# GNN kernel: fewer sorted tiles, their leftovers packed into gathered steps (100 sorted and 320 gathered steps a pass)

## The chip, the cores and the metric

The kernel runs on one core of one Trainium2 chip. The metric is the device time of one execution in microseconds (us). The kernel before took 2686.7 us (median of 3 runs, 2684.65 to 2692.53).

## The reference, cut to what matters

There are 3125 nodes with 128 features and 50000 directed edges, sorted by destination. Sources are uniform; destinations are `3125 * u**2`, so low nodes get many edges. First a gated network runs five steps over the graph, then a layer norm. Then three edge layers run, and it is these that the change touches:

```python
def _gnn_layer(edge_index, x, edge_attr, norm, We, be, Wn, bn):
    src, dst = (edge_index[0], edge_index[1])
    parts = [x[src], x[dst]]
    if edge_attr is not None:
        parts.append(edge_attr)
    e = relu(concatenate(parts, axis=-1) @ We + be)
    msg = e * norm[:, None]
    agg = segment_sum(msg, dst, num_segments=x.shape[0])
    x_new = relu(concatenate([x, agg], axis=-1) @ Wn + bn)
    return (x_new, e)
x, e = _gnn_layer(edge_index, z, None, norm, We0, be0, Wn0, bn0)
x, e = _gnn_layer(edge_index, x, e, norm, We1, be1, Wn1, bn1)
x, e = _gnn_layer(edge_index, x, e, norm, We2, be2, Wn2, bn2)
```

A second layer norm of the result plus its input is the output.

## The kernel before, in words

Nodes are cut into 25 windows of 128. Edges are cut into tiles of 128 and, since they are sorted by destination, each piece of a tile that falls into one destination window is a **step**; there is room for 416 steps. `x[src] @ We_a` and `x[dst] @ We_b` are made once per node in a node stage (P and Q); P goes to memory as `p_dram`, and both stay on the chip as three bfloat16 parts (`p_parts`, `q_parts`).

An **edge pass** (`edge_pass`, one per layer, called pass 0, 1 and 2 here) works in slots of four steps (`QUAD`). There are two kinds of slot.

- A **gathered** slot, here R, covers the later steps. GpSimd fetches P's row of every edge by an indirect DMA, one per step (L1496), into one of 7 row buffers. TensorE adds Q by a one-hot matrix, 3 matmuls a step (L1585), VectorE adds the gathered rows (`add`, L1714), ScalarE applies relu (L1657).
- A **sorted** slot, here S, covers tiles whose edges share both the source window and the destination window. Their P comes from the chip too: 3 matmuls a step with the source's one-hot matrix (L1578) and 3 with the destination's (L1585), so nothing is gathered. VectorE makes both one-hot matrices of the four tiles in one operation (`paired_hot`, L1695), and relu reads the PSUM bank.

Passes 1 and 2 also add the previous layer's e times a weight (L1589, 2 matmul records a step); passes 0 and 1 turn e and store it (L1600). Every slot ends with a weighted one-hot product per step (`turn_and_sum`, L1607), which VectorE adds to the destination window's sums (`gather_up`, L1721). TensorE's order is written out: the products of slot q, then the turning and summing of slot q-1. VectorE's is: `add` of slot q (or the pair of one-hots of the next sorted slot), then `gather_up` of slot q-1 with the weighted one-hots of slot q+1 between. A row buffer is given back when the slot that used it is summed, and only then does GpSimd gather into it.

The kernel before has 38 sorted slots and 76 gathered ones in the fixed order S R R, so 114 slots a pass. The windows' numbers that the matmuls need are read into registers once in three slots (`lists`, L1469).

Which edge goes to which sorted tile is worked out at the start (`sort_on_dve` and its matmuls in `step_tables`): the first 112 steps are counted by source window and destination window (a block), every block gets as many tiles as it needs, rounded up, and each edge's place is the first place of its block plus its rank (`block_rank`, summed by L340). The places are used by an indirect scatter in the next stage (L625). The register loads, the table loads and the one-hot rows of the first steps follow in `node_stage`. If the sorted tiles did not suffice, a loop at the end of each pass (`overflow`, L1503 and on) would treat further tiles one by one.

## Time and profile before

| | |
|---|---|
| median of 3 runs | 2686.7 us |
| the profiled execution, its own time | 2711.26 us |
| its span, first to last instruction | 2709.1 us |
| TensorE matmul busy | 2123.5 us (78%) |
| VectorE busy | 1447.8 us (53%) |
| GpSimd busy | 1068.0 us (39%) |
| ScalarE busy | 675.5 us (25%) |
| mean granted TensorE clock | 0.880 |

The stages by the profile: tables and sorting 0 to 70 us, the adjacency matrix 70 to 400, the gated steps to 938, a layer norm and the first node stage to some 1022, then pass 0 to 1513, pass 1 to some 2115, pass 2 to 2670, each followed by a node stage. Busy shares are averages over these stages. Matmul records are modelled at their end, so a busy TensorE is not one at its peak, and an idle engine costs nothing unless another waits for it.

### The profile page before, as it was taken

How to read it: one execution, taken by the hardware profiler on the slowest of the kernel's cores; microseconds unless marked ns; L12 is line 12 of the kernel's file. 1: busy time of each engine (PE TensorE's matmuls, PEld its weight loads, DVE VectorE, ACT ScalarE, POOL GpSimd, SP SyncE). 2: the span in 40 equal slices, each digit the busy share in tenths (PEclk: the TensorE clock that was granted, in tenths of full speed). 3: DMA queues.
4: the chain of work that ended last, by engine and by line, in shares of the span. 5: the costliest groups of instructions: out<-in, count | busy, mean ns of one | idle time of the engine just before them, and what ended most of it. 6: DMA issues, size and time to landing. Idle time of an engine off the chain costs nothing. (4 is left out here: it accounts for less than half of the span.)

```text
span 2709.1 us, 50361 instructions
## 1 busy us (share of the span) xinstructions
PE 2123.5 (78%) x14516; PEld 1514.4 (56%) x14516; DVE 1447.8 (53%) x4548; ACT 675.5 (25%) x1344; POOL 1068.0 (39%) x1086
## 2 busy tenths in 40 slices
PE   7777769999999726777777558888889458888885
PEld 5112124444444425666776348877878357777773
DVE  6888751322323255666666425555556336566565
ACT  0245751221212131222222312222222301111111
POOL 0544410000000035666664165555553266666650
PEclk7667779999999867889788769999999679999997
DMA  2023560000000043434443135555554134444431
GB/s 80 21 59 72 88 64 1 0 0 0 0 0 0 24 175 116 119 115 118 116 117 110 46 107 166 167 166 166 170 168 159 53 88 115 117 118 117 120 110 38
DMA packets 188937, 242.82 MB, mean 90 GB/s; under 512 B 53218, under 2 KB 115069, under 8 KB 188077
## 3 DMA queue, kind: packets, MB, share of 16 engines
q1 hardware_dynamic: 155852, 179.60, 22.9%
q0 software_dynamic: 32864, 60.32, 9.3%
q8 instruction: 135, 2.21, 0.3%
q14 instruction: 86, 0.70, 0.1%
HBM read 150.92 MB, written 69.26 MB: 81 GB/s over the span
## 5 line engine op out<-in xcount | busy, mean ns | idle before, releaser
L1496 POOL DMA_INDIRECT rows<-p_dram,src_i x912 | 899.4, 986 | 561.1 <-PE psum L1607 230.5
L1721 DVE TENSOR_TENSOR agg_t<-psum,agg_t 128x128 f32 x1368 | 390.8, 286 | 493.9 <-PE psum L1607 208.2
L1589 PE MATMUL psum<-w_c,before 128*128 128x128 f32 x1824 | 419.3, 310 | 18.9 <-issue 18.6
L882 PE MATMUL psum<-adj,parts 128*128 (+2 forms) x1750 | 340.0, 352 | 5.3 <-ACT agg L961 4.4
L1705 DVE TENSOR_SCALAR hot_w<-col_f,dst_loc,weight 128x128 f32<-128x128 f32 x912 | 323.9, 357 | 0.3
L1657 ACT ACTIVATE rows<-rows 128x512 f32<-128x512 f32 x228 | 143.6, 630 | 720.1 <-DVE rows L1714 459.7
L1585 PE MATMUL psum<-q_parts,hot_all 128*128 x2736 | 283.4, 221 | 29.3 <-issue 28.4
L1589 PEld LDWEIGHTS psum<-w_c,before 128*128 128x128 f32 x1824 | 289.3, 199 | 22.2 <-issue 22.2
L662 PE MATMUL psum<-src_hot,dst_hot 128*128 128x391 f16 x586 | 230.7, 439 | 77.5 <-ACT psum L684 26.7
L1607 PE MATMUL psum<-hot_w,rows 128*128 128x128 f32 x1824 | 270.2, 292 | 26.5 <-issue 24.9
L1578 PE MATMUL psum<-p_parts,pair_hot 128*128 x1368 | 194.2, 245 | 105.5 <-DMA before<-e_dram 49.4
L1262 POOL MEMSET agg_t<- 128x3200 f32 x3 | 8.3, 2765 | 664.4 <-POOLq L1010 607.4
L1607 PEld LDWEIGHTS psum<-hot_w,rows 128*128 128x128 f32 x1824 | 243.4, 205 | 33.8 <-issue 30.3
L882 PEld LDWEIGHTS psum<-adj,parts 128*128 128x128 f16 x1750 | 153.2, 98 | 190.9 <-issue 23.7
L1585 PEld LDWEIGHTS psum<-q_parts,hot_all 128*128 128x128 bf16 x2736 | 219.6, 99 | 51.9 <-issue 39.4
L1585 PE MATMUL psum<-q_parts,pair_hot 128*128 x1368 | 225.5, 246 | 15.6 <-issue 14.9
L1714 DVE TENSOR_TENSOR rows<-psum,rows 128x512 f32<-128x512 f32 x228 | 156.6, 687 | 138.5 <-remote 119.9
L1578 PEld LDWEIGHTS psum<-p_parts,pair_hot 128*128 128x128 bf16 x1368 | 134.5, 109 | 140.3 <-issue 121.8
L830 DVE SCALAR_TENSOR_TENSOR gate_room<-psum,b_h,gate_room 128x512 f32<-128x512 f32 (+1 forms) x35 | 23.9, 683 | 348.9 <-ACT gate_room L968 348.9
L662 PEld LDWEIGHTS psum<-src_hot,dst_hot 128*128 128x128 f16 x586 | 59.2, 101 | 249.1 <-issue 249.1
L644 DVE TENSOR_SCALAR src_hot<-gate_room 128x391 f16<-128x391 f16 x586 | 167.7, 332 | 53.2 <-PE psum L662 39.9
L625 POOL DMA_INDIRECT records<-record_of,place_i x112 | 125.6, 1122 | 158.6 <-PE psum L662 158.1
(248 smaller groups left out, 2547.2 us busy)
## 6 DMA issues: line engine op xcount, KB each, us to landing
e_dram<-after SPq DMA_DIRECT2D x228, 256.0 KB
before<-e_dram SPq DMA_DIRECT2D x228, 256.0 KB
adj<-stage SPq DMA_DIRECT2D x196, 97.8 KB
pair_rows<-sorted_rows SPq DMA_DIRECT2D x114, 128.0 KB
rows<-p_dram,src_i POOLq DMA_INDIRECT x912
hot_all<-dst_rows SPq DMA_DIRECT2D x1, 3584.0 KB
hot_all<-dst_rows SPq DMA_DIRECT2D x1, 3072.0 KB
hot_all<-dst_rows SPq DMA_DIRECT2D x1, 2048.0 KB, 7.5
```

The lines of the kernel that those rows point to most:

```text
L644: nc.vector.tensor_scalar(src_hot[:, s % MOVES, :], span_h, place_f[:, s:s + 1], None, ALU.is_equal).then_inc(src_on, 1)
L662: nc.tensor.matmul(psum[:, bass.ds(bank, 1), 0:SPAN], dst_hot[:, s // HOT_BATCH % BATCHES, s % HOT_BATCH, :], src_hot[:, s % MOVES, :], st ...
L882: mm = nc.tensor.matmul(psum[:, AGG_BANK, 0:n_cols], parts[:, w, part, :], adj[:, w, cols], start=(w == 0 and part == 0), stop=(w == WINDO ...
L1496: nc.gpsimd.indirect_dma_start(out=rows[:, b % ROWS, m * D:(m + 1) * D], out_offset=None, in_=p_dram, in_offset=bass.IndirectOffsetOnAxis( ...
L1578: nc.tensor.matmul(o, hots[0], t["p_parts"][:, bass.ds(values[m], 1), part, :], start=(part == 0), stop=False)
L1585: mm = nc.tensor.matmul(o, hot, t["q_parts"][:, bass.ds(window, 1), part, :], start=(part == 0 and i is None), stop=(part == 2 and e_befor ...
L1589: mm = nc.tensor.matmul(o, before[:, q % BEFORE, m * P:(m + 1) * P], w_c[:], start=False, stop=True)
L1607: mm = nc.tensor.matmul(psum[:, A_BANKS[q % len(A_BANKS)], m * P:(m + 1) * P], e[:, m * D:(m + 1) * D], hot_w[:, q % 2, m, :], start=True, ...
L1657: nc.scalar.activation(e_of(q), source, ACT.Relu).then_inc(e_on, 1)
L1705: nc.vector.tensor_scalar(hot_w[:, q % 2, m, :], keep["col_f"][:], of, weight, ALU.is_equal, ALU.mult).then_inc(hot_on, 1)
L1714: nc.vector.tensor_tensor(row, psum[:, E_BANKS[q % len(E_BANKS)], 0:WIDE], row, ALU.add).then_inc(added, 1)
L1721: nc.vector.tensor_tensor(a, psum[:, A_BANKS[q % len(A_BANKS)], m * P:(m + 1) * P], a, ALU.add).then_inc(agg_on, 1)
```

## The change

Only the first 104 steps are sorted. A block now gets full tiles, and one more if 64 edges or more are left over; fewer than 64 are left out of the sorted tiles. What is left out of all blocks of one destination window is packed side by side into tiles of that window, 8 tiles in all (`LEFT_TILES`), which are treated as gathered steps. So a pass has 25 sorted slots and 80 gathered ones (312 of the steps as before, plus the 8 packed tiles), 105 in all. They are mixed evenly: of each 21 slots 5 are sorted, with 4, 3, 3, 3 and 3 gathered slots behind them.

For this the sorting gives every edge two keys instead of one (the first tile of its block with its rank, and where its leftovers start with how many tiles its block fills), takes them apart with shifts and masks, and chooses the place. The window numbers are in two tables now, read once in two sorted slots and once in four gathered ones.

```diff
-SORT_STEPS = 112
-SORT_QUADS = 38
+SORT_STEPS = 104
+SORT_QUADS = 25
 SORT_TILES = SORT_QUADS * QUAD
-REST_STEPS = STEPS - SORT_STEPS
+LEFT_TILES = 8
+HELD_TILES = LEFT_TILES + SORT_TILES
+FULL_FROM = 64
+REST_STEPS = STEPS - SORT_STEPS + LEFT_TILES
-ALL_TILES = 737
+ALL_TILES = 236
+RANKS, FILLS = 14, 9
...
     dve.wait_ge(block_sizes, 1)
-    after(nc.vector.tensor_scalar(tiles_i[0:W, :], psum[...], float(P - 1), None, ALU.add))
+    after(nc.vector.tensor_scalar(tiles_i[0:W, :], sizes, float(P - FULL_FROM), None, ALU.add))
     after(nc.vector.tensor_scalar(tiles_i[0:W, :], tiles_i[0:W, :], 7, None, ALU.logical_shift_right))
     after(nc.vector.tensor_copy(tiles_f[0:W, :], tiles_i[0:W, :]))
+    after(nc.vector.scalar_tensor_tensor(out=left[0:W, :], in0=tiles_f[0:W, :], scalar=-float(P), in1=sizes, ...))
+    after(nc.vector.tensor_scalar(left[0:W, :], left[0:W, :], 0.0, None, ALU.max))
+    v.on(nc.vector.tensor_reduce(row_sums[0:W, 0:1], tiles_f[0:W, 0:W], AXIS_X, ALU.add))
+    after(nc.vector.tensor_reduce(row_sums[0:W, 1:2], left[0:W, 0:W], AXIS_X, ALU.add))
+    after(nc.vector.tensor_scalar(left_i[0:W, :], row_sums[0:W, 1:2], float(P - 1), None, ALU.add))
+    after(nc.vector.tensor_scalar(left_i[0:W, :], left_i[0:W, :], 7, None, ALU.logical_shift_right))
+    v.on(nc.vector.tensor_copy(left_tiles[0:W, :], left_i[0:W, :]))
...
+    for key in range(2):
+        if key:
+            dve.wait_ge(vec, done["rank_key0"])
         for i, a in enumerate(range(0, W, CHAINED)):
             ...
+        done[f"rank_key{key}"] = v.on(nc.vector.tensor_reduce(
+            rank_key[:, key, :], block_rank[:].rearrange("p k s -> p s k"), AXIS_X, ALU.add))
+    after(nc.vector.tensor_copy(key_i[:], rank_key[:]))
+    ... (20 more operations of 128 x 104, most of which wait for the one before)
     v.on(nc.vector.tensor_tensor(keep["place_i"][:], place[:], spare[:], ALU.add))
...
     pe.wait_ge(vec, done["step_base"])
-    for i in range(chains):
-        a, n, _ = below(i)
-        for k in range(n):
-            mm = nc.tensor.matmul(psum[:, i, k * S:(k + 1) * S], row_of[:, a + k, :],
-                                  step_base[0:W, :], start=False, stop=(k == n - 1))
+    for key in range(2):
+        for i in range(chains):
+            a, n, _ = below(i)
+            ...
+            for k in range(n):
+                mm = nc.tensor.matmul(psum[:, j % CHAIN_BANKS, k * S:(k + 1) * S], row_of[:, a + k, :],
+                                      step_base[0:W, key, :], start=(key == 1), stop=(key == 1 or k == n - 1))
...
     # the first node stage
+    sp.wait_ge(tabs, 80)
     for i in range(1, len(HOT_CHUNKS) - 1):
         load_hot(sp, i)
...
+    dve.wait_ge(keep["sorted_got"], 16)
+    for to, f in ((t["src_i"], 3), (t["dst_loc"], 1), (t["weight"], 2)):
+        nc.vector.tensor_copy(to[:, STEPS - SORT_STEPS:REST_STEPS],
+                              keep["sorted_in"][:, 0:LEFT_TILES, f]).then_inc(turned_on, 1)
...
     # the edge pass
+    order, nth_of = [], []
+    for q in range(SLOTS):
+        kind = q * SORT_QUADS % SLOTS < SORT_QUADS
+        nth_of.append(order.count(kind))
+        order.append(kind)
+    slots = {kind: [q for q in range(SLOTS) if order[q] == kind] for kind in (True, False)}
+    AT_A_TIME = {True: 2, False: 4}
...
+    def lists(values, q, engine):
+        i, n = nth_of[q], AT_A_TIME[order[q]]
+        if i % n == 0:
+            ... (16 values from pair_i or rest_i)
...
-                if q >= len(E_BANKS) and i is not None:
+                if q >= len(E_BANKS) and order[q - len(E_BANKS)]:
                     pe.wait_ge(e_on, q - len(E_BANKS) + 1)
```

## Rows read from the trace of the kernel before

**Rows 1.** Windows: busy of PE, PEld, DVE, ACT, POOL, clock, DMA share, GB/s.

```profile
52.00:64.00 12.00, 11.65 (x57) 11.44 (x58) 9.31 (x34) 0.00 (x0) 0.00 (x0) 0.50 0.00 0
...
1037.00:1505.00 468.00, 357.34 (x3156) 322.39 (x3156) 304.60 (x1090) 129.32 (x227) 276.35 (x276) 0.86 0.39 114
...
1575.00:2104.00 529.00, 446.26 (x4053) 407.38 (x4053) 285.94 (x1020) 127.86 (x228) 285.35 (x293) 0.94 0.53 158
...
2190.00:2662.00 472.00, 386.04 (x3584) 344.61 (x3583) 284.71 (x1016) 69.96 (x113) 274.93 (x279) 0.98 0.39 111
```

**Rows 2.** Source line L1657, relus of gathered slots, passes 0, 1, 2: min/median/max ns.

```profile
L1657 ACT ACTIVATE rows<-rows x76: 629/629/631, 1037.1 to 1499.1; 128x512 f32<-128x512 f32 x76
...
L1657 ACT ACTIVATE rows<-rows x76: 629/630/632, 1601.0 to 2096.0; 128x512 f32<-128x512 f32 x76
...
L1657 ACT ACTIVATE rows<-rows x76: 629/630/633, 2198.2 to 2656.8; 128x512 f32<-128x512 f32 x76
```

**Rows 3.** Timeline of TensorE, slots in passes 0, 1, 2: start us, us, work.

```profile
1304.50 0.53 PE L1578 MATMUL psum<-p_parts,pair_hot 128*128 x3
...
1308.04 0.83 PE L1585 MATMUL psum<-q_parts,hot_all 128*128 x12
...
1316.02 0.53 PE L1578 MATMUL psum<-p_parts,pair_hot 128*128 x3
...
1320.64 0.83 PE L1585 MATMUL psum<-q_parts,hot_all 128*128 x12
...
1329.54 0.53 PE L1578 MATMUL psum<-p_parts,pair_hot 128*128 x3
...
1862.51 0.56 PE L1578 MATMUL psum<-p_parts,pair_hot 128*128 x3 [0.62 <-issue]
...
1867.20 0.33 PE L1585 MATMUL psum<-q_parts,hot_all 128*128 x3
...
1875.65 0.57 PE L1578 MATMUL psum<-p_parts,pair_hot 128*128 x3 [0.46 <-DMA before<-e_dram]
...
2412.39 0.48 PE L1578 MATMUL psum<-p_parts,pair_hot 128*128 x3 [0.26 <-issue]
...
2417.30 0.33 PE L1585 MATMUL psum<-q_parts,hot_all 128*128 x3
...
2424.85 0.35 PE L1578 MATMUL psum<-p_parts,pair_hot 128*128 x2 [0.23 <-issue]
```

**Rows 4.** Waits between 1050 and 1480 us: total us, times, longest us.

```profile
POOL rows L1496 <- PE psum L1607: 74.6, 54, 1.8
POOL rows L1496 <- issue: 62.5, 204, 0.4
```

**Rows 5.** Source line L1496, the gathers of pass 0.

```profile
L1496 POOL DMA_INDIRECT rows<-p_dram,src_i x303: 938/944/1402, 999.7 to 1472.1; - x152
```

**Rows 6.** Timeline in pass 0, a gather beside the pair of one-hots.

```profile
1307.56 0.74 DVE L1695 TENSOR_SCALAR pair_hot<-pair_rows,lane_f 128x1024 bf16<-128x1024 uint8 x1
1307.72 1.39 POOL L1496 DMA_INDIRECT rows<-p_dram,src_i  x1 [0.30 <-issue]
```

**Rows 7.** Source line L1469, the loads of window numbers into registers.

```profile
L1469 PEldq TENSOR_LOAD <-list_i x114: 1101/1106/1882, 997.8 to 2645.6; - x114
```

**Rows 8.** Timeline of the sorting, 39 to 68 us.

```profile
39.52 0.27 DVE L280 SCALAR_TENSOR_TENSOR valid<-dst_e,inside 128x112 f32<-128x112 f32 x1
39.82 0.27 DVE L282 SCALAR_TENSOR_TENSOR src_key<-src_win,valid 128x112 f16<-128x112 int32 x1
...
52.35 11.00 PE L543 MATMUL psum<-step_base,row_of 25*128 25x112 f32 x50 [0.35 <-DVE step_base L327]
...
63.80 4.85 DVE L340 TENSOR_REDUCE place<-block_rank 128x112 f32<-128x2800 f32 x1
```

**Rows 9.** Timeline behind pass 0: the last sums, then the node stage.

```profile
1501.47 1.59 DVE L1721 TENSOR_TENSOR agg_t<-psum,agg_t 128x128 f32 x4 [0.91 <-PE psum L1607]
...
1513.02 0.29 DVE L1770 TENSOR_TENSOR agg_t<-psum,agg_t 128x128 f32 x1 [1.45 <-PE psum L1640]
```

More of the change, by code:

```diff
@@ new lines, in sort_on_dve @@
+            after(nc.vector.tensor_scalar(at_i[:, 2, :], at_i[:, 0, :], P - 1, None, ALU.bitwise_and))
+            after(nc.vector.tensor_tensor(tile_f[:], base[:], at_i[:, 1, :], ALU.add))
+            after(nc.vector.tensor_scalar(shift_f[:], tile_f[:], float(LEFT_TILES), past[:, 1:2], ALU.is_ge, ALU.mult))
+            after(nc.vector.scalar_tensor_tensor(out=shift_f[:], in0=shift_f[:], scalar=-float(LEFT_TILES),
+                                                 in1=is_left[:], op0=ALU.add, op1=ALU.mult))
@@ L1453, in edge_pass, with pair_slot @@
         E_BANKS, T_BANKS, A_BANKS = (0, 1, 2), (3, 4), (5, 6, 7)
+        order, nth_of = [], []
[5 more added lines that the diff above has]
+        AT_A_TIME = {True: 2, False: 4}
         def sorted_of(q):
-            return q // 3 if q % 3 == 0 else None
+            return nth_of[q] if order[q] else None
         def rest_of(q):
-            return q // 3 * 2 + q % 3 - 1
+            return nth_of[q]
         def slot_of(b):
-            return b // 2 * 3 + b % 2 + 1
-        def lists(i, first, engine):
-            _, values = nc.values_load_multi_w_load_instructions(
-                keep["list_i"][0:1, i, first:4 * QUAD], engines=(engine,), min_val=0, max_val=WINDOWS - 1,
-                skip_runtime_bounds_check_because="a window's number is a count of at most all the windows but one")
-            return values
+            return slots[False][b]
+        def pair_slot(i):
+            return slots[True][i]
+        def lists(values, q, engine):
+            i, n = nth_of[q], AT_A_TIME[order[q]]
+            if i % n == 0:
+                if order[q]:
+                    table = keep["pair_i"][0:1, i:min(i + n, SORT_QUADS), :, :].rearrange("p i f m -> p (i f m)")
+                else:
+                    table = keep["rest_i"][0:1, i * QUAD:min(i + n, REST_QUADS) * QUAD]
+                _, values[order[q]] = nc.values_load_multi_w_load_instructions(
+                    table, engines=(engine,), min_val=0, max_val=WINDOWS - 1,
+                    skip_runtime_bounds_check_because="a window's number is a count of at most all the windows but one")
+            per = 2 * QUAD if order[q] else QUAD
+            return values[order[q]][i % n * per:(i % n + 1) * per]
         def overflow(engine):
             return nc.values_load(keep["over_i"][0:1, 0:1], engines=(engine,), min_val=0,
-                                  max_val=ALL_TILES - SORT_TILES)
+                                  max_val=ALL_TILES - HELD_TILES)
         def over_window(engine):
@@ L1730, in _ @@
                     weighted_hot(q, m)
+            loaded = {}
             for q in range(SLOTS):
```

204 lines of the change are left out of this document (135 added, 69 removed).

## The prediction, made before the result was known

> **What bounds the kernel now.** I read the page first: its span by stages says that three edge passes take some 1470 us of 2709, and the change reaches little else. Then the windows of the passes [rows 1]: the busiest engine in each is TensorE (357 of 468 us, 446 of 529, 386 of 472), with GpSimd behind it. GpSimd's busy time leaves out the issue gap between gathers. One gather is 276.35/276 = 1.00 us in pass 0 and 0.97 to 0.99 in the others [rows 1], and 62.5/204 = 0.31 us passes before most [rows 4], so a gathered slot takes GpSimd 4 x 1.31 = 5.2 us in pass 0 and 4 x 1.29 = 5.15 in the others. In each triple S R R that is 10.4 us of about 12.4, and the rest it waits for a row buffer, that is for TensorE's sums (74.6 us in 430) [rows 4]. So the gathers follow the slots and don't set their pace. TensorE's in-order stream, with VectorE's adds and ScalarE's relus hung into it, does.
>
> The pace comes from the relus of the gathered slots [rows 2]. The first is slot 1 and the last slot 113, 112 slots apart: 462.0/112 = 4.13 us a slot in pass 0, 495.0/112 = 4.42 in pass 1, 458.6/112 = 4.09 in pass 2. The 15 to 40 us before the first of them (first rows and tables) don't depend on the slots' number.
>
> **What a slot of each kind costs** is to be read from where TensorE starts its products [rows 3]. From the start of S to that of the next R is S's share; from there to the next S are two R. Pass 0: S 3.54 and 4.62, mean 4.08; R (7.98 + 8.90)/4 = 4.22. Pass 1: S 4.69, R 8.45/2 = 4.23. Pass 2: S 4.91, R 7.55/2 = 3.78. The sums 12.5, 13.1 and 12.5 agree with three times the pace. A sorted slot has 12 more matmuls than a gathered one, so it is a little dearer where TensorE is fullest.
>
> **The passes.** Each loses 13 S and gains 4 R.
> - Pass 0: -13 x 4.08 + 4 x 4.22 = -36.2 us.
> - Pass 1: -13 x 4.69 + 4 x 4.23 = -44.1.
> - Pass 2: -13 x 4.91 + 4 x 3.78 = -48.7.
>
> Together -129.0. With the mean slot instead (9 fewer at 4.13, 4.42, 4.09) it would be -113.8; I take the split, because TensorE's products are what differs.
>
> Does GpSimd keep up? In 21 slots there will be 16 gathered ones: 16 x 5.2 = 83 us of gathers against 5 x 4.08 + 16 x 4.22 = 88 us of slots in pass 0, 82 against 91 in pass 1, 82 against 85 in pass 2. It does, with 3 to 10% left. The longest run is 4 gathered slots and there are 7 buffers, so a run is served out of what was fetched during the sorted slot before it. The whole of pass 0's 320 gathers takes 320 x 1.31 = 419 us from its first issue at 999.7 [rows 5], so to 1419; the forecast end of the pass is about 1465. That lead of GpSimd is the cover; the rivals say what it costs if it is gone.
>
> VectorE: 304.6 us busy in 468 [rows 1]; a gathered slot gives it an add instead of a pair of one-hots, about the same, and 9 slots fewer a pass. ScalarE is at 28%. The SP queue issues 9 fewer stores and loads of e a pass and 13 fewer pair loads. Loads of window numbers [rows 7], 1.10 us each on TensorE's queue: 13 + 20 = 33 a pass instead of 38, beside the sums already issued; I count nothing (a bound: 15 fewer x 1.1 = 16 us gained if none is hidden). VectorE reads 16 numbers now instead of 12, in time when it waits for sums. TensorE's wait for the slot three before now asks for relu only where the bank held a sorted slot; it never waits longer than before.
>
> **The sorting** is on the path: the next stage begins only when it has ended. The 50 matmul records of L543 took 11.0 us [rows 8] at a granted clock of 0.50 [rows 1], 1.2 GHz, though TensorE was busy 11.65 of 12 us. There will be 100 of 104 columns, about 20.5: +9.5 to 11, I take 10.2. A second reduction (4.85 us) [rows 8] runs after them, the first is hidden beneath them: -0.35 for the smaller size. Behind it 22 more VectorE operations. Two dependent ones start 0.30 apart [rows 8]; some 15 wait so, the rest at about half: 5.1. Ahead of the matmuls seven more small operations on the block sizes, three small products and two more base products, each at 0.1 to 0.3: 2.9. In sum +17.9, I say +17.5; from 12 (if the clock rises in the longer run) to 23.
>
> **The rest** costs nothing by its cover: the scatter has 104 steps instead of 112 inside a stage that TensorE and VectorE fill; zeroing the records falls from 737 tiles to 236, beside the sorting; three small copies in the first node stage fall into VectorE's wait for the first products; SP's new wait for five small tables stands behind four stores of P issued much later; the last chunk of one-hot rows is 0.5 MB longer and needed half a pass later. If the covers failed, I put 5 us on them together.
>
> **The overflow loop** ran one turn behind each pass: the profile has its last sum after pass 0 [rows 9]. A count over the reference's edges (seed 0) gives 146 sorted tiles of 152 now, so its body runs once even with nothing left over. For the change the same count gives 99 full tiles of 100 and 880 edges left, which pack into 8 tiles of 8. So one turn again, no difference.
>
> **Sum**, against the profiled execution: 2711.3 - 129.0 + 17.5 = 2599.8 us. The median of the runs is 0.9909 of that execution; the same share gives 2576.
>
> **Rivals.**
> - *A sorted slot costs others more than its own time.* Its 24 products stand in TensorE's order before the sum that frees a row buffer and that VectorE waits for. If this delay is what makes the R behind it dear, R falls too. The floor is GpSimd: 16 x 5.15 us in 21 slots, 3.92 a slot, 404 us for 103 slots, against 462, 495 and 459 today: -204. Half way between forecast and floor is -166, so 2711 - 166 + 17 = 2562, 2539 as a median. For it: pass 0 had R's between 3.6 and 6.9 apart in two neighbouring triples. Against: with this many R's GpSimd's waits would have to vanish altogether.
> - *The sorted slot was GpSimd's breathing space.* 5 to 10% is little left; if buffers come late in each run and half the gain is lost in waits for rows, the passes give -65: 2711 - 65 + 17 = 2663, 2639.
> - *The gathers become the bound: slower.* Place: GpSimd, beside VectorE's one-hots. A gather that ran beside the pair of one-hots took 1.39 us instead of 0.94 [rows 5, 6]. If all did, one would be 1.39 + 0.31 = 1.70 and a pass 544 us, against 1472.1 - 999.7 = 472 now: +72 a pass, +216 + 17, about 2917. It decides from 472/320 = 1.48 us a gather on; 1.31 is measured. The pairs become fewer by a third, the weighted one-hots stay at four a slot. Against it: the median gather is 944 ns with VectorE 65% busy [rows 1, 5].
> - *The clock.* It is 0.86 granted in pass 0 and 0.94 and 0.98 in the others [rows 1]. Fewer products a slot leave TensorE emptier. If passes 1 and 2 fell to 0.86, their TensorE time, 446 and 386 us before, would be longer by 9% and 14%: after the cut about +37 and +47, half of it on the path, +42: 2642, 2618 as a median.
> - *More overflow* (the count wrong): each tile over costs one more turn, 1513.31 - 1503.06 = 10.3 us [rows 9], three times a run, +31; four such tiles would eat the gain.
>
> Two rules of the Trainium skill speak against the change. "SBUF — State Buffer", section "SBUF: two separate sides", says that GpSimd can't write the descriptors of a DMA while VectorE runs an operation that takes the port pair they share. By that rule each of the weighted one-hots would hold the gathers up, which is the third rival at its full price; the one long gather beside the pair agrees, the median doesn't. "TensorE: Matmul & The Clock Gate", Part 1, says that an idle TensorE falls to half its clock; by it the fourth rival is the case to fear, and pass 0, the emptiest pass, has the lowest clock. By the same rule the sorting's matmuls would have run at full clock once busy; the row at 0.50 shows that they didn't.
>
> **How the numbers follow.** The forecast, 2545 to 2610, has 0.55. The dearer sorted slot has 0.20, the lost breathing space 0.10, the clock 0.08, gathers as the bound 0.05, more overflow 0.02 (half of it still faster). Predicted: 2576. The range is to hold 8 in 10: its low end, 2525, takes in three quarters of the first rival; its high end, 2635, takes in the clock and half of the breathing space. A measurement of this kernel can tell about 0.3% (8 us) from no change. Slower are gathers as the bound 0.05 and half of more overflow 0.01, so 0.06; 0.02 of the breathing space and the clock I give to no measurable change, and the rest, 0.92, is faster.
>
> **What would show it.** Relus of gathered slots: 80 a pass, from the first to the last about 426, 451 and 410 us, a slot at 4.0 to 4.4. GpSimd's waits for L1607 down to a fifth; gathers at 0.94 to 1.0 us, 960 of them. The scatter's first piece at 91 us instead of 73.5, since the stage begins so much later. One turn of the overflow loop a pass. Wrong would be: VectorE's add waiting for rows most of the time, a clock under 0.9 in pass 2, or gathers at a median above 1.2 us.

## The result, and the profile after

The kernel after takes 2755.9 us (median of 4 runs, 2752.33 to 2758.83), beside 2685.8 (2684.65 to 2692.53) for the kernel before: the ratio is 1.0249 [1.0235, 1.0263], slower. The forecast was 2576, range 2525 to 2635. The profiled executions are 2711.26 and 2752.33 us, so the trace explains 41 us of the 70; the rest is that the profiled execution of before was 1% above its median and that of after 0.1% below.

One thing has to be known first. The 18 experiments ran in five groups, each on a chip of its own beside the kernel before. In three groups (e, f, h) that kernel took 2383 to 2385 us, in two (g, k) 2713 to 2714, and in the result 2686. All executions of it in one group agree. So there are two conditions of the machine, called **prompt** (2384) and **late** (2686 to 2714) here. Whether they belong to the chip or to the hour isn't known, since no chip was used twice. The result is of the late one, and so is the profile that the prediction rests on. The change is slower in both.

Windows of the kernel after, with the columns of [rows 1]: the sorting, then passes 0, 1 and 2.

```profile
52.00:68.00 16.00, 15.54 (x72) 14.64 (x72) 10.94 (x38) 0.00 (x0) 0.00 (x0) 0.50 0.00 1
1054.00:1531.00 477.00, 345.09 (x2774) 298.43 (x2774) 281.21 (x1006) 115.44 (x208) 283.25 (x292) 0.82 0.35 104
1609.00:2111.00 502.00, 410.06 (x3596) 367.16 (x3596) 259.85 (x927) 117.37 (x208) 296.24 (x307) 0.94 0.52 154
2200.00:2699.00 499.00, 394.19 (x3180) 349.99 (x3180) 261.18 (x928) 64.87 (x105) 286.52 (x298) 0.85 0.36 100
```

TensorE has 9 slots fewer than in [rows 1] and is busy for 345, 410 and 394 us instead of 357, 446 and 386; in pass 2 it is busy longer with less to do, at a granted clock of 0.85 instead of 0.98. The relus of gathered slots, as in [rows 2], show what that means for the passes.

```profile
L1772 ACT ACTIVATE rows<-rows x80: 629/629/631, 1055.1 to 1530.6; 128x512 f32<-128x512 f32 x80
L1772 ACT ACTIVATE rows<-rows x80: 629/630/632, 1631.9 to 2110.8; 128x512 f32<-128x512 f32 x80
L1772 ACT ACTIVATE rows<-rows x80: 629/630/632, 2211.8 to 2698.8; 128x512 f32<-128x512 f32 x80
```

| first to last such relu, us | pass 0 | pass 1 | pass 2 | sum |
|---|---|---|---|---|
| before [rows 2] | 462.0 | 495.0 | 458.6 | 1415.6 |
| after, forecast | 426 | 451 | 410 | 1287 |
| after | 475.5 | 478.9 | 487.0 | 1441.4 |
| us a slot (before 112, after 103 intervals) | 4.13 to 4.62 | 4.42 to 4.65 | 4.09 to 4.73 | |

The rest is as forecast: the first of them begins 18.0 us later than before, and what lies between and behind the passes is 2.4 us shorter. So 18.0 + 25.8 - 2.4 = 41.4 us, the difference of the spans (2750.5 and 2709.1).

The gathers in the view of the line and in the waits between 1050 and 1480 us, the counterparts of [rows 4, 5]:

```profile
L1612 POOL DMA_INDIRECT rows<-p_dram,src_i x960: 938/944/1509, 1016.4 to 2673.4; - x192
...
POOL rows L1612 <- issue: 69.7, 228, 0.4
POOL rows L1612 <- PE psum L1723: 49.6, 21, 9.8
POOL rows L1612 <- remote: 45.0, 25, 2.3
DVE rows L1829 <- PE psum L1701: 16.2, 9, 10.2
```

A gather costs what it did, 944 ns at the median. GpSimd still waits for row buffers, 49.6 + 45.0 = 94.6 us in 46 pauses, though more rows are wanted. In before it was 74.6 us [rows 4] and one more line of that view, together 89.7 us in 68 pauses:

```profile
POOL rows L1496 <- remote: 15.1, 14, 1.4
```

The longest wait of an add for TensorE is 10.2 us, which is two slots.

**Where TensorE's results are.** One place of pass 0 in after, by engine. First TensorE:

```profile
1160.36 0.83 PE L1701 MATMUL psum<-q_parts,hot_all 128*128 x12
...
1164.80 0.47 PE L1701 MATMUL psum<-q_parts,pair_hot 128*128 x3
1166.47 0.22 PE L1694 MATMUL psum<-p_parts,pair_hot 128*128 x1 [1.20 <-issue]
1167.19 0.22 PE L1694 MATMUL psum<-p_parts,pair_hot 128*128 x1 [0.50 <-issue]
1167.91 0.22 PE L1694 MATMUL psum<-p_parts,pair_hot 128*128 x1 [0.50 <-issue]
1169.29 0.46 PE L1701 MATMUL psum<-q_parts,pair_hot 128*128 x3 [1.16 <-issue]
```

The timeline of VectorE, the adds, and then of GpSimd:

```profile
1160.74 0.68 DVE L1829 TENSOR_TENSOR rows<-psum,rows 128x512 f32<-128x512 f32 x1
1169.36 0.69 DVE L1829 TENSOR_TENSOR rows<-psum,rows 128x512 f32<-128x512 f32 x1 [5.87 <-remote]
```

```profile
1157.96 0.94 POOL L1612 DMA_INDIRECT rows<-p_dram,src_i  x1 [1.54 <-PE psum L1723]
1159.20 0.94 POOL L1612 DMA_INDIRECT rows<-p_dram,src_i  x1 [0.30 <-issue]
...
1165.44 0.94 POOL L1612 DMA_INDIRECT rows<-p_dram,src_i  x1 [0.30 <-issue]
1166.69 0.95 POOL L1612 DMA_INDIRECT rows<-p_dram,src_i  x1 [0.30 <-issue]
1169.76 0.94 POOL L1612 DMA_INDIRECT rows<-p_dram,src_i  x1 [2.12 <-remote]
```

The twelve products of a gathered slot are recorded as done at 1161.19. The add that reads them begins at 1169.36, 8.2 us later, with VectorE idle for 5.87 us before it. In that time GpSimd issues eight gathers without a pause, 1157.96 to 1167.64, and TensorE's next matmuls start only every 0.72 us, though nothing that the profile shows holds them. When the eight are issued, all moves again. I call it a slow stretch when three or more times in a row the next matmul starts at least 0.55 us after the last, with no wait for another engine. After has 20, 3 and 13 of them in passes 0, 1 and 2; before has 2, 1 and 1, at the passes' starts. The matmuls' record and their reader's start lie up to 9.0 us apart in after and up to 5.5 in before; in the mean, without the first seven gathered slots of a pass, it is 2.3 us in after and 3.0 in before. So results are late in before too, and more evenly.

In before GpSimd pauses after each four. Its timeline:

```profile
1149.31 0.94 POOL L1496 DMA_INDIRECT rows<-p_dram,src_i  x1 [1.03 <-PE psum L1607]
1150.55 0.94 POOL L1496 DMA_INDIRECT rows<-p_dram,src_i  x1 [0.31 <-issue]
1151.80 0.96 POOL L1496 DMA_INDIRECT rows<-p_dram,src_i  x1 [0.30 <-issue]
1153.06 0.94 POOL L1496 DMA_INDIRECT rows<-p_dram,src_i  x1 [0.30 <-issue]
1155.62 0.94 POOL L1496 DMA_INDIRECT rows<-p_dram,src_i  x1 [1.61 <-PE psum L1607]
```

In after, behind the 28 gathers that need not wait for a buffer, 24 series of pass 0, none of pass 1 and 13 of pass 2 have eight. How this is tied to the slots' time is what the experiments ask.

### The profile page after: what moved, and what is told of

Read it like the earlier page. It is cut to its first block and busy times, and to the rows that moved or that the text cites. A ratio compares the mean times of both kernels' runs of the same rounds, so it can differ in the third digit from the quotient of the medians.

```text
span 2750.5 us, 46647 instructions
## 1 busy us (share of the span) xinstructions
PE 2092.9 (76%) x13351; PEld 1467.4 (53%) x13351; DVE 1396.1 (51%) x4356; ACT 648.6 (24%) x1299; POOL 1087.8 (40%) x1126
## 5 line engine op out<-in xcount | busy, mean ns | idle before, releaser
L1612 POOL DMA_INDIRECT rows<-p_dram,src_i x960 | 927.9, 967 | 568.9 <-issue 238.3
L1836 DVE TENSOR_TENSOR agg_t<-psum,agg_t 128x128 f32 x1260 | 357.1, 283 | 519.0 <-DMA records<-pad 180.9
L1701 PE MATMUL psum<-q_parts,hot_all 128*128 x2880 | 346.8, 240 | 105.7 <-issue 94.6
L1723 PE MATMUL psum<-hot_w,rows 128*128 128x128 f32 x1920 | 304.5, 295 | 76.3 <-issue 65.9
L1701 PEld LDWEIGHTS psum<-q_parts,hot_all 128*128 128x128 bf16 x2880 | 260.5, 109 | 158.0 <-issue 138.4
L1820 DVE TENSOR_SCALAR hot_w<-col_f,dst_loc,weight 128x128 f32<-128x128 f32 x960 | 336.6, 353 | 0.8
L1723 PEld LDWEIGHTS psum<-hot_w,rows 128*128 128x128 f32 x1920 | 264.4, 207 | 94.6 <-issue 83.7
L1694 PE MATMUL psum<-p_parts,pair_hot 128*128 x900 | 120.5, 231 | 98.1 <-issue 63.4
L1772 ACT ACTIVATE own<-psum 128x512 f32<-128x512 f32 x75 | 44.8, 597 | 480.6 <-remote 419.0
L1716 PE MATMUL psum<-ident,rows 128*128 128x128 f32 x640 | 110.6, 299 | 58.9 <-ACT rows L1772 40.2
(300 smaller groups left out, 2423.0 us busy)
```

Source lines behind the costliest of these rows:

```text
L1612: nc.gpsimd.indirect_dma_start(out=rows[:, b % ROWS, m * D:(m + 1) * D], out_offset=None, in_=p_dram, in_offset=bass.IndirectOffsetOnAxis( ...
L1694: nc.tensor.matmul(o, hots[0], t["p_parts"][:, bass.ds(values[m], 1), part, :], start=(part == 0), stop=False)
L1701: mm = nc.tensor.matmul(o, hot, t["q_parts"][:, bass.ds(window, 1), part, :], start=(part == 0 and i is None), stop=(part == 2 and e_befor ...
L1723: mm = nc.tensor.matmul(psum[:, A_BANKS[q % len(A_BANKS)], m * P:(m + 1) * P], e[:, m * D:(m + 1) * D], hot_w[:, q % 2, m, :], start=True, ...
L1772: nc.scalar.activation(e_of(q), source, ACT.Relu).then_inc(e_on, 1)
L1820: nc.vector.tensor_scalar(hot_w[:, q % 2, m, :], keep["col_f"][:], of, weight, ALU.is_equal, ALU.mult).then_inc(hot_on, 1)
```

## The experiments

Gathered relus, first to last in each pass, stand behind each time. Ratios are to before on the same chip. A time without a ratio is of one execution. "Old rows" means that the add takes what lies in the row buffer.

### Group e, prompt machine (before 2383.4)

**e1**: the kernel after in the order S R R as long as there are sorted slots, then 30 R.

```diff
-            kind = q * SORT_QUADS % SLOTS < SORT_QUADS
+            kind = q % 3 == 0 and q < 3 * SORT_QUADS
```

> What is tested: in the kernel after the change TensorE has stretches, about one to each sorted slot in passes 0 and 2, in which one matmul starts only every 0.70 to 0.72 us with no wait on anything the profile shows. Here only the order of the slots changes: S R R 25 times (75 slots, the order of the kernel before), then the other 30 gathered slots in one run. Theory order (a run of three or four gathered slots lets TensorE's stream fall into such a stretch at the next sorted slot): the first 75 slots of a pass go at 4.1 to 4.4 us each as before, and the passes lose about what I forecast, so 2590 to 2640 us. Theory loads (the window numbers are now read into registers at other places and times than once ahead of each triple): the order is not the cause, the stretches stay, 2730 to 2770 us. Theory gathers (more gathers a slot disturb TensorE): the stretches gather in the last 30 slots, which then take over 5 us each; in sum 2700 to 2770.

Measured: 2423.0, ratio 1.0171 [1.0154, 1.0188]; 379.5, 397.1, 394.6. That is the time of after itself on a prompt machine (f2 below, 2420.7), so the order is worth nothing here. All three ranges that were expected had a late machine in view.

**e2**: TensorE takes window numbers fixed in the program, so it loads no registers.

```diff
-                products(q, lists(loaded, q, mybir.EngineType.PE))
+                products(q, [4 * (q % 5) + m for m in range(2 * QUAD)])
```

> The kernel after, with TensorE's products reading a window of P and Q that is fixed in the program instead of one from a register, so that TensorE's queue has neither the register loads nor the register operations of the passes; the products have the same sizes, but are with the wrong windows. If the stretches hang on the registers (theory loads, or the sequencer's register work in general), they are gone and the passes take at most 3.9 us a slot: 2450 to 2600 us. If they come from the order or from the gathers, they stay: 2700 to 2760 us.

Measured: 2420.7; 381.8, 396.2, 395.4. Nothing again.

**e3**: only the first 7 gathered slots of a pass fetch rows (84 gathers in all, later slots add old rows).

```diff
-            for b in range(REST_QUADS):
-                if b >= ROWS:
-                    pool.wait_ge(summed, slot_of(b - ROWS) + 1)
+            for b in range(ROWS):
```

> The kernel after, in which GpSimd gathers only the first seven slots of each pass; the later gathered slots work on what lies in the row buffers. The 960 gathers become 84. Theory gathers: the stretches go, and a slot takes 4 us or less: 2550 to 2620 us. Theories order and loads: they stay, and since the rows landed some 30 us ahead anyway the time is within 1% of 2756 us.

Measured: 2217.2; 311.1, 350.4, 304.8. So 200 us lie with the gathers.

**e4**: the kernel before with its window numbers loaded by kind, as after does (two sorted or four gathered slots at once).

> The kernel before, with one part of the change alone: the window numbers are read into registers as the kernel after does it (8 for each of two sorted slots at once, 4 for each of four gathered slots at once, each time where the first of them is used) instead of 16 once ahead of each S R R. Nothing else is changed; 38 loads a pass become 38 (19 and 19). Theory loads: the stretches appear here too and the kernel gets slower by 50 us or more, 2730 to 2800 us. Theory order or gathers: within 0.5% of 2686 us.

Measured: 2377.6, 0.9974 [0.9964, 0.9985]; 364.3, 395.4, 378.3. The one part of the change that gains, 6 us by the medians. In the traces it is pass 1 that gets shorter (395.4 against 408.7 in f1). It was not run on a late machine.

### Group f, prompt machine (before 2385.1): the four corners

**f1** and **f2** are before and after unchanged; **f3** and **f4** are before and after with e3's edit.

> The kernel before, unchanged, for its trace beside the others of this group. In the first group it ran at 2383 us, 300 us faster than in the runs that the prediction rests on, and the traces there show GpSimd issuing one gather every 1.25 us without a break. Theory gathers (where TensorE's products end as soon as their records say, the gathers set the pace: 304 x 1.25 = 380 us a pass): the time is about 2383 us, passes of 368, 400 and 381 us from the first relu to the last, GpSimd waiting under 20 us for TensorE in all three. If it falls into the condition of the first runs instead: 2686 us, slots of 4.1 to 4.6 us, and matmuls whose results come up to 5 us after their records.

> The kernel after, unchanged. Theory gathers: 320 x 1.25 = 400 us a pass, 16 more gathers are +20 us a pass where they bound already (passes 0 and 2), in pass 1 less, and +18 us for the sorting: 2420 to 2435 us beside 2383, ratio 1.016 to 1.022. Theory stretches (slow stretches of TensorE at the sorted slots are what costs, wherever it runs): ratio 1.025 with such stretches in the trace. My forecast of 0.96 would need the passes to follow TensorE's slots.

> The kernel before, gathering only the first seven slots of each pass (84 gathers instead of 912). With the same edit of the kernel after (passes of 314.6, 353.2 and 307.8 us for 25 sorted and 80 gathered slots) it gives the price of a slot to TensorE and VectorE alone. With a sorted slot at 3.0 to 3.5 us and a gathered one at about 2.9: 38 and 76 slots take 330 to 355 us in passes 0 and 2 and 380 to 395 in pass 1, so 2250 to 2310 us. If the gathers did not bound the kernel before, its time would not fall by more than 20 us.

> The kernel after with 84 gathers instead of 960, once more, beside the kernels of this group. Theory gathers: 2217 us again, and 30 to 80 us below the kernel before with the same edit, which is what the change would give if the gathers cost nothing. In the condition of the first runs it tells whether the gathers are what makes TensorE's results late: then slots of 3.0 to 3.4 us; if not, slots of 4.5 us or more.

| | pass 0 | pass 1 | pass 2 | time | 
|---|---|---|---|---|
| f1 before | 363.5 | 408.7 | 379.9 | 2384.4 |
| f2 after | 379.5 | 394.5 | 395.6 | 2420.7, ratio 1.0154 [1.0137, 1.0171] |
| f3 before, few gathers | 358.5 | 403.5 | 345.4 | 2341.1 |
| f4 after, few gathers | 311.2 | 349.9 | 306.0 | 2219.0 |

Without the gathers the change gives its passes 1107.4 - 967.1 = 140 us back, where 129 was forecast. With them the passes get 1169.6 - 1152.1 = 17.5 us longer, and the sorting adds its 18. The waits of f2 in the whole span (us, times, longest) say why, and a stretch of GpSimd's timeline beside them:

```profile
POOL rows L1612 <- issue: 282.8, 928, 0.3
DVE rows L1829 <- DMA rows<-p_dram,src_i: 258.4, 151, 4.3
```

```profile
1147.35 0.94 POOL L1612 DMA_INDIRECT rows<-p_dram,src_i  x1 [0.30 <-issue]
1148.60 0.94 POOL L1612 DMA_INDIRECT rows<-p_dram,src_i  x1 [0.30 <-issue]
1149.85 0.95 POOL L1612 DMA_INDIRECT rows<-p_dram,src_i  x1 [0.30 <-issue]
```

GpSimd waits for no buffer: 928 of 960 gathers follow the one before at once. One begins every 1.25 us (0.94 + 0.31), so a gathered slot costs 5.0 us whatever TensorE does, and 79 x 5.0 = 395 us is the pass: 379.5 (the first gathers lie ahead of the first relu), 394.5, 395.6. In f1 the adds waited for rows 44 times, 80.5 us; in f2 151 times.

### Group g, late machine (before 2714.2)

**g1**: before with a spare gather (into a tile that nobody reads) after every 19, so 16 more a pass, the number that the change adds. The dots stand for a wait until the spare gather before it has landed.

```diff
+                    if s % 19 == 18:
+                        ...
+                        nc.gpsimd.indirect_dma_start(
+                            out=spare_rows[:], out_offset=None, in_=p_dram, ...).then_inc(spare_in, 16)
```

> The kernel before with 16 more gathers in each pass (one more after every 19, of rows that nothing uses): 320 a pass instead of 304, as the kernel after has, and nothing else. Theory gathers (GpSimd's stream of gathers at 1.25 us each is what ends last): +20 us in pass 2, where the kernel before followed the gathers (383 us against 348 us with few of them), +10 to 20 in pass 0 (366 against 361), 0 to 5 in pass 1 (411 against 407): 2384 becomes 2410 to 2430, ratio 1.011 to 1.019. Theory slots (the pace is TensorE's, the gathers follow): within 0.3% of 2384. Should the group meet the condition of the first runs, where the rows lay ready some 30 us before they were used: no change of 2686.

Measured: 2779.6, ratio 1.0268 [1.022, 1.0316]; 482.0, 515.3, 481.7. 48 gathers cost 65 us, 1.36 us each, though GpSimd had waited 74.6 us in pass 0 alone [rows 4] and nobody reads these rows. It had been expected that a late machine would show no change. The waits between 1050 and 1480 us are still there:

```profile
POOL rows L1498 <- PE psum L1617: 63.5, 47, 1.8
POOL rows L1498 <- remote: 23.9, 17, 2.3
```

That is 87.4 us beside 89.7 in before. The added gathers did not go into the waits, they came on top.

**g2**: after with 16 gathers fewer a pass: the slots with b % 20 == 19 add old rows.

```diff
-                for m in range(QUAD):
+                for m in range(0 if b % 20 == 19 else QUAD):
```

> The kernel after without the gathers of four of its 80 gathered slots a pass (they add the products to what lies in the row buffer): 304 gathers instead of 320. All else is the change as it is, its sorting, its 25 sorted and 80 gathered slots. Theory gathers: 16 x 1.25 = 20 us less in each of the three passes, since each is bound by them: 2421 becomes 2360 to 2372, ratio to before 0.989 to 0.995. So the change would be a small gain if it did not add gathers. Theory slots: 2415 to 2425.

Measured: 2746.4, 1.0116 [1.0092, 1.0141]; 474.5, 479.7, 480.1. By ratio this is 0.0133 x 2700 = 36 us of the 70, but the time is only 9.5 us below that of after and its passes 7 (1434.3 against 1441.4). So taking 48 gathers away gives back 7 to 36 us here, where adding 48 cost 65. The slow stretches (15, 1, 11) and the series of eight (22, 0, 10) mostly stay.

**g3**: after, but from the eighth gathered slot on only two of four rows are fetched (522 gathers; the rest old rows).

> The kernel after with two of the four gathers of a gathered slot (174 a pass instead of 320). Theory gathers: GpSimd needs 218 us a pass, so TensorE sets the pace and the time is that of 28 gathers a pass, 2219 us within 10 us: past the crossing the number of gathers costs nothing, and that GpSimd and VectorE work side by side costs TensorE's stream nothing either. If gathers slow the other engines even when they are not the pace: half way, about 2320 us.

Measured: 2309.2; 315.3, 358.1, 320.3. GpSimd's waits in g3:

```profile
POOL rows L1612 <- PE psum L1723: 447.0, 217, 9.6
```

It issues two, waits, issues two; one slow stretch is left, at the start of pass 2, and from the products' record to the add it is 1.1 us in the mean, against 2.3 in after. The time lies near the 2320 us that was expected if gathers slow the others even where they are not the pace. 438 gathers fewer gave 2755.9 - 2309.2 = 447 us (two chips, so within some 30).

**g4**: e2 and e3 together.

> The kernel after with 28 gathers a pass and, on TensorE, windows that are fixed in the program (no register loads, no register operations). It asks what sets TensorE's pace once the gathers are out of the way (3.02, 3.40 and 2.96 us a slot). From the two kernels with few gathers a sorted slot costs 4.3 us in pass 0 and a gathered one 2.6. If the register operations, one every 0.12 us and 24 of them in a sorted slot, make the sorted slot dear: it falls to 3 us or less, 25 x 1.3 x 3 = 100 us off 2219, 2100 to 2140 us. If VectorE's adds and one-hots do: within 20 us of 2219.

Measured: 2224.5; 284.8, 337.1, 307.1. With few gathers the late machine is as fast as the prompt one (e3 2217). Two stretches are left, both where the 28 gathers of a pass are issued in a row.

### Group h, prompt machine (before 2383.7)

**h1**: after without gathers; SP loads four plain blocks of 128 rows of P for each gathered slot instead, as many bytes.

```diff
+                    sp.dma_start(rows[:, b % ROWS, m * D:(m + 1) * D],
+                                 p_dram[w * P:(w + 1) * P, :]).then_inc(rows_in[b % ROWS], 16)
```

> The kernel after without gathers: the 80 gathered slots of a pass get their rows by plain loads of 128 whole rows of P each (not the rows that the edges name), four a slot, from the SP queue; 320 transfers a pass and 64 KB each stay, GpSimd issues none. Where the group meets the late TensorE of the first runs: if it is the bytes that move (through memory and the transfer engines) that make TensorE's results late, the time stays near that of the change, 2700 us or more; if it is GpSimd's issuing of gathers (their descriptors), TensorE is on time and it takes 2250 to 2350 us. Where TensorE is on time anyway: 2219 to 2300 us, since the gathers' pace of 1.25 us is gone.

Measured: 2286.8; 310.9, 389.1, 302.8. Passes 0 and 2 are as in f4; only pass 1, where SP also stores and loads e, pays.

**h3**: after with `ROW_SLOTS = 4`, so that GpSimd can't run ahead.

> The kernel after with four row buffers instead of seven, so that GpSimd can't issue more than 16 gathers ahead of TensorE's sums and pauses more often. If long unbroken series of gathers are what throws TensorE into the slow stretches, they become rarer and the time falls below that of the change by 30 us or more in the late condition. If every gather costs TensorE the same wherever it lies: within 15 us of the change. Where TensorE is on time, the gathers are the pace and less cover costs 0 to 40 us more than 2421.

Measured: 2449.9; 395.0, 396.1, 394.2. Passes 1 and 2 unmoved: 79 x 5.0 again. On a late machine, where the question arose, it was not run.

**h4**: every gather takes the index column 0 (the same 128 rows each time).

> The kernel after, with every gather taking the rows that the first column of indices names (the same 128 rows of P each time), so that the number of gathers, descriptors and bytes stays and only the spread of the addresses in memory goes. If scattered reads of memory make TensorE late (or set the gather's time), 100 us or more less than the change; if descriptors do, the same within 15 us in either condition.

Measured: 2419.6; 379.3, 395.6, 393.7. Which rows are fetched doesn't matter on a prompt machine; on a late one it was not run.

**h5** is e1 once more.

> The kernel after in the order S R R 25 times, then 30 gathered slots, as in the first group, where it ran at a ratio of 1.017 with TensorE on time. In the late condition: if the order of the change (three or four gathered slots in a row) causes the slow stretches, the 75 slots in triples have none and the time is 40 us or more below that of the change, with stretches in the last 30 slots alone. If the number of gathers alone counts: a ratio of 1.02 to 1.03, as the change has.

Measured: 2427.5, 1.0178 [1.0161, 1.0195]; 381.1, 398.1, 394.7, as e1.

### Group k, late machine (before 2712.9)

**k1** is e1 on a late machine.

> The kernel after in the order S R R 25 times and then 30 gathered slots, a third time, for the case that this group meets the late TensorE of the result. There: if the runs of three and four gathered slots cause the slow stretches (one at nearly every sorted slot), the triples have none, the ratio falls from 1.025 to 1.01 or below, and the stretches that remain stand in the last 30 slots; if only the number of gathers counts, 1.02 to 1.03. Where TensorE is on time: 1.017 again.

Measured: 2736.5 (2736.13 to 2738.87), ratio 1.0089 [1.0072, 1.0106]; 464.5, 493.8, 464.2. Here the order counts: after in its own order has 1.0249. g2, with 48 gathers fewer and beside the same before (2714.2 and 2712.9), takes 9.9 us longer than k1. In k1 both rhythms stand in one pass. Windows of its triples and of its last R's, in passes 0 and 2:

```profile
1080.00:1330.00 250.00, 191.38 (x1686) 168.62 (x1685) 163.22 (x580) 67.47 (x119) 158.62 (x161) 0.90 0.39 117
1400.00:1520.00 120.00, 71.44 (x541) 67.19 (x541) 62.23 (x220) 24.52 (x44) 69.82 (x74) 0.73 0.30 91
2250.00:2500.00 250.00, 207.29 (x1921) 182.68 (x1919) 151.99 (x540) 37.14 (x60) 156.43 (x161) 1.00 0.41 117
2550.00:2680.00 130.00, 96.33 (x665) 85.82 (x664) 60.14 (x216) 15.11 (x24) 77.97 (x82) 0.79 0.32 89
```

In the triples GpSimd issues 0.64 gathers a us (161 in 250) in series of four and TensorE's clock is 0.90 and 1.00. In the tails, with nothing but gathered slots, it issues 74 in 120 and 82 in 130 (68 in the first 100 us of either, since the last gather starts at 1508.5 and 2670.6), the clock is 0.73 and 0.79, and TensorE is busy 60% and 74% instead of 77% and 83%. The last 30 gathered relus of each pass are 5.44, 5.50 and 5.42 us apart. In pass 1 this tail has series of four. GpSimd's timeline in the tail of pass 0 shows the cycle, with the eighth gather of a series ahead of the next one:

```profile
1430.02 0.94 POOL L1612 DMA_INDIRECT rows<-p_dram,src_i  x1 [0.30 <-issue]
1433.18 0.94 POOL L1612 DMA_INDIRECT rows<-p_dram,src_i  x1 [2.21 <-remote]
...
1441.91 0.94 POOL L1612 DMA_INDIRECT rows<-p_dram,src_i  x1 [0.30 <-issue]
1445.11 0.94 POOL L1612 DMA_INDIRECT rows<-p_dram,src_i  x1 [2.26 <-remote]
```

Eight gathers, 2.2 us of pause, eight gathers: 11.9 us for two slots (1433.18 to 1445.11), which is 1.49 us a gather. Of pass 2's 11 slow stretches 9 lie in the tail, but pass 0's tail has none and the same pace.

**k2** is h1 on a late machine.

> The kernel after with plain loads of whole rows from the SP queue in place of the gathers, for the same case. With TensorE on time it took 2287 us. In the late condition: 2700 us or more if the bytes make TensorE late; 2250 to 2350 us if GpSimd's issuing of gathers does.

Measured: 2287.5; 311.8, 389.2, 302.9: the numbers of h1, on a chip where before is 330 us slower, and no slow stretch. GpSimd has next to nothing to issue in k2; its line on the page:

```profile
PE 1900.5 (83%) x13351; PEld 1343.1 (59%) x13351; DVE 1393.2 (61%) x4356; ACT 646.9 (28%) x1299; POOL 159.9 (7%) x166
```

So neither the bytes of the rows nor any other work makes a machine late. The gathers that GpSimd issues do. k2 takes away their issuing and their scattered reads together; h4, which keeps the first and takes away the second, ran on a prompt machine alone.

### GpSimd's time in a pass, from the traces

From the start of the 29th gather of a pass, the first that needs a buffer back, to the end of the last, GpSimd either issues or pauses. A pause here is idle time beyond the 0.3 us that stand between any two gathers. All three passes together, us:

| | 29th to last gather | issuing | pauses (times) | last gather to last relu | passes |
|---|---|---|---|---|---|
| before, late | 1321.5 | 1044.0 | 277.5 (207) | 80.3 | 1415.6 |
| g1, 48 more gathers | 1385.4 | 1098.3 | 287.0 (205) | 79.4 | 1479.0 |
| after, late | 1359.9 | 1088.5 | 271.4 (182) | 68.8 | 1441.4 |
| k1, after in the order S R R | 1368.4 | 1088.2 | 280.1 (195) | 43.1 | 1422.5 |
| f1, before, prompt | 1067.7 | 1061.6 | 6.1 (10) | 34.4 | 1152.1 |
| f2, after, prompt | 1112.0 | 1112.0 | 0 | 9.0 | 1169.6 |

(What is missing to the passes lies between the first relu and the 29th gather: 11 to 14 us late, 49 to 50 prompt.) On a late machine 48 more gathers add their issuing, 54 us in g1 and 44 in after, and the pauses hardly move. A series of eight in after has a longer pause than a series of four, 2.0 us against 1.4 beyond the 0.3, but one for eight gathers: 1.50 us a gather against 1.59. So it delays results longest and still costs no more.

## Why the prediction was wrong

**The cause.** A gathered slot has four gathers, and they are its price, not TensorE's products. On a prompt machine directly: GpSimd is never idle and a slot waits for its rows. On a late one through TensorE, as the traces read: while GpSimd issues gathers, TensorE's results come late, the sum that frees a buffer is late with them, and GpSimd then waits for that buffer. So each series of gathers is followed by a pause, and a pass is issuing plus pauses plus what lies behind the last gather. The chain of waits names TensorE, and the true bound is behind it. That gathers cost this time is shown by adding and removing them (g1, g3, g4, k2); that it goes by way of TensorE is read from the timelines. A series of eight keeps itself up: two slots finish at once and free two buffers at once. The change takes away slots without gathers and adds slots with four.

By the steps of the prediction:

- **What bounds the passes: failed, and this decides.** It read GpSimd's waits for L1607 as "so the gathers follow the slots and don't set their pace". g1 refutes it: 48 more gathers, 65 us, and the waits as long as before. With its pauses GpSimd already took (1472.1 - 999.7)/304 = 1.55 us a gather in before and (1507.6 - 1016.4)/320 = 1.54 in after; 1.31 leaves out pauses that never went away.
- **Price of each kind, read between TensorE's records: failed.** S 4.08, 4.69, 4.91 and R 4.22, 4.23, 3.78, from two triples of pass 0 and one of each other pass. In k1, R's without any S take 5.44, 5.50 and 5.42. An estimate from that: with three slots at the pace of [rows 2], S = 12.39 - 10.88 = 1.5, 13.26 - 11.00 = 2.3, 12.27 - 10.84 = 1.4. A sorted slot is nearly free, since it falls into time in which gathers are issued anyway. The same sum with these prices gives +2.3, -7.9 and +3.5 us, -2 in all, instead of -129. That is 127 of the 155 us by which the passes missed. The prices were in the old trace only as a mixture; the positions of modelled records split it wrongly. Where gathers are taken away the sorted slot is dear after all (f3 and f4, 140 us), so the forecast's -129 would nearly have fitted a kernel without gathers.
- **The remaining 28 us (25.8 measured against -2): 19 are the order, by way of the passes' ends.** k1's passes sum to 1422.5, after's to 1441.4. The other 9 are k1's own distance from the estimate (+7 against -2). The ratios (1.0249 and 1.0089) would make the order up to 43 us, but the before of the result ran faster than that of k1. By pass after takes 11.0 us more, 14.9 less and 22.8 more. The table says where: up to the last gather after is 8.5 us *shorter* than k1 in sum, behind it 25.7 us longer, and 1.6 longer ahead of the 29th. Behind the last gather the rows lie ready, and in the change's own order nine slots are left there, two of them sorted, in k1 seven gathered ones. So the sorted slots that stand last are not hidden under gathers. The series of eight, which this order brings, are not what costs. On the prompt machine, where the last rows come in just ahead of their adds, e1 and h5 show the order at nothing.
- **"Does GpSimd keep up": the sum was close and the conclusion wrong.** It took 5.2 and 5.15 us per gathered slot; 5.0 is measured on a prompt machine. On the prompt machine GpSimd is full all the same, since the slots take less than the 4.0 to 4.7 us that it was set against (f4: 3.0, 3.4 and 3.0): "3 to 10% left" between two estimates was no cover. On the late one it does keep up, 80 us of gathers (16 x 5.0) in 21 slots of 4.62 us or 97, but only because the gathers themselves make the slots long.
- **Sorting +17.5: right.** The scatter's first piece starts at 91.57 instead of 73.54 us, +18.0:

```profile
54.41 21.66 PE L633 MATMUL psum<-step_base,row_of 25*128 25x104 f32 x100 [0.46 <-DVE step_base L364]
...
76.48 5.02 DVE L386 TENSOR_REDUCE rank_key<-block_rank 128x104 f32<-128x2600 f32 x1
...
86.80 0.27 DVE L417 TENSOR_TENSOR place_i<-place,spare 128x104 int32<-128x104 f32 x1
...
91.57 1.19 POOL L717 DMA_INDIRECT records<-record_of,place_i  x1 [0.19 <-issue]
```

  The matmuls begin 2.1 us later (2.9 forecast) and took 10.7 more (10.2 forecast), the reduction is 0.2 longer instead of 0.35 shorter, and from its end to the scatter it is 10.07 us instead of 4.89, so 5.2 more (5.1 forecast).
- **Register loads at nothing: right for the change** (e2 is within 1 us of f2). e4 has them at -6 in before, so "nothing" is not exact. With few gathers they are worth 38 us of a late machine's passes (967.1 in f4 against 929.0 in g4, two machines).
- **One turn of the overflow loop: right.** Its sum in after:

```profile
1544.78 0.29 DVE L1885 TENSOR_TENSOR agg_t<-psum,agg_t 128x128 f32 x1 [1.45 <-PE psum L1755]
```

- **The factor 0.9909 from the profiled execution to the median: wrong.** It is a matter of one execution of before, whose 2711 us lie with the 2713 to 2714 of groups g and k and not with the 2685 to 2693 of its own runs. The profiled execution of after has no such surplus. Without the factor the forecast would have been 24 us higher (2599.8 instead of 2576), still on the wrong side.
- **Rivals.** *The gathers become the bound* (0.05) was right in place and sign and wrong in its price: it wanted dearer gathers (1.48 us and more, 2917 us), but the median stayed at 944 ns, and it is their number that costs. *Breathing space* (0.10, 2639) named what f2 shows, adds that wait for rows, but let half of the gain stand; nothing of it stood. On the late machine the adds wait for results and not for rows. *The clock* did fall, to 0.82 and 0.85, in passes 0 and 2, and did so where gathered slots alone leave TensorE emptier (k1: 0.90 and 1.00 in the triples, 0.73 and 0.79 in the tails). It does so without any pause of GpSimd too: 0.94 and 0.95 in passes 0 and 2 of f2, where f1 has 1.00. How much it gives back in turn wasn't separated. *A dearer sorted slot* had the wrong sign wherever gathers run.

The rule of "SBUF — State Buffer" in the Trainium skill that was weighed, GpSimd held up by VectorE, is not borne out for the weighted one-hots, beside which a gather keeps its median of 944 ns. All 42 gathers of after's passes above 1.2 us overlap a pair of one-hots, as the one of [rows 6] did. What costs here goes another way, from GpSimd to TensorE. That the record of a matmul ends by estimate is said in the Trainium skill, "Perfetto Trace Analysis", section "Tensor Engine Instruction (MATMUL, LD_WEIGHTS)"; the trace agrees, with 8.2 us between such an end and the reader.

**Open.** By what path gathers hold TensorE's results back, whether that is the issuing or the scattered reads, and what makes one machine late and another prompt, no run shows. The best kernel seen is e4, 0.26% below before on a prompt machine. A version with the change's slots and without its gathers would be worth up to 200 us (f2 to f4), but P's rows must come from somewhere: h1 and k2 show the price of moving them by plain loads, not a way to address them.

## What to carry to other kernels

Price a step by the resource that it alone uses, counted at its own rate (here 4 gathers of 1.25 us), before you price it by the pace of a mixture; work that hides under another's bound is cheap to keep, and removing it buys nothing. A wait for TensorE at the end of a chain is no proof that TensorE is the bound: ask whether its result came when its record ends, and add or remove a few units of the other suspect, which decided it here in one run. Idle time that stays when work is added is no slack. And ask of each end of a pass what still hides under the bound there.

## What the runs showed of the hardware that was not expected

- The same kernel takes 2384 us on three chips and 2686 to 2714 in the other runs; without gathers a machine of each kind takes the same (h1 2286.8, k2 2287.5).
- While GpSimd issues eight gathers in a row (10 us), a late machine's TensorE at times starts a matmul only every 0.72 us and its results come up to 9.0 us behind their records; per gather this costs no more than series of four (1.50 us against 1.59). An unread spare gather costs 1.36 us there, though GpSimd had idle time.
- One gather of 128 rows of 512 bytes holds GpSimd for 0.94 us with 0.31 us to the next, whichever rows it fetches (h4).
- TensorE, 97% busy for 16 us in the sorting (15.54 us), was granted 0.50, its lower level, 1.2 GHz. The lower level had begun at 42.9 us, when it had been idle for 5.2 us.
